# Ranking in PSUM, full-width matmuls and a single grid instruction in an early-fusion kernel

## The reference

```
h = concat(tokens(x), txt)                       # 192 x 64 for each of 16 examples
h = h + softmax(LN(h) LN(h)^T / 8) LN(h)
z = LN(h); w = z wr + br                         # router: one number per token
sel = the 95 tokens with the largest w           # top 96, of which 95 are used
h = h + z + [w * (gelu(z w1 + b1) w2 + b2) for tokens in sel, 0 elsewhere]
h = h + causal attention of 16 heads of 64, one key head, window 128, RoPE, RMS norm
z = LN(h); e = argmax(z rout + rb)               # one of 32 experts
h = h + relu(relu(z W1[e] + b1[e]) W2[e] + b2[e])
```

## Time and profile before

| | us |
|---|---|
| median of 3 runs (579.9 to 582.99) | 582.66 |
| the profiled execution | 583.62 |
| its span, first to last instruction | 581.8 |
| PE busy, of the span | 502.2 (86%) |
| DVE busy | 417.8 (72%) |
| ACT busy | 311.9 (54%) |
| POOL busy | 234.7 (40%) |
| granted TensorE clock, mean | 0.971 |

### The profile page before, as it was taken

How to read it: one execution, slowest core, us unless ns; L and a number is a source line. 1 busy time by engine, 2 the same in 40 slices (tenths; PEclk the granted TensorE clock), 3 DMA queues, 4 the chain that set the end, 5 groups by cost and what they waited for, 6 DMA issues and landing times.

```text
span 581.8 us, 14569 instructions
## 1 busy us (share of the span) xinstructions
PE 502.2 (86%) x5920; PEld 386.4 (66%) x5920; DVE 417.8 (72%) x1291; ACT 311.9 (54%) x593; POOL 234.7 (40%) x217
## 2 busy tenths in 40 slices
PE   3457499879999899989998999899989999899845
PEld 2235277658867786778776877688767767777622
DVE  3669766996799769976997699957995697363220
ACT  1414346565667556766577565756575655454311
POOL 2316632554446342643454436354462446420000
PEclk9999999989999999999998999899999999999966
DMA  7000000000000000000000000000000000000000
GB/s 271 1 6 0 1 7 2 3 1 7 3 2 10 7 2 2 10 7 3 2 9 3 2 3 2 8 3 2 3 10 2 2 2 9 2 3 9 2 1 7
DMA packets 6450, 6.29 MB, mean 11 GB/s; under 512 B 4208, under 2 KB 5744, under 8 KB 6256
## 3 DMA queue, kind: packets, MB, share of 16 engines
q1 hardware_dynamic: 6384, 5.37, 3.0%
HBM read 4.31 MB, written 0.79 MB: 9 GB/s over the span
## 4 chain that ended last, share of the span: by engine, by line
PE 47%; DVE 35%; ACT 9%; POOL 2%; issue 2%; DMA 2%; SPq 1%; POOLq 0%; ACTq 0%; DVEq 0%
PE bank L961 38%; PE bank L979 10%; DVE eq L515 5%; DVE negm L631 4%; DVE q_sb L568 4%; DVE ssq L585 4%; DVE tb L568 4%; DVE on L648 3%; ACT qT L810 3%; POOL qs L793 2%; DMA p<-masks 2%; DVE eq L506 1%; ACT qs L810 1%; DVE eq L431 1%; DVE rec L644 1%
## 5 line engine op out<-in xcount | busy, mean ns | idle before, releaser
L631 DVE TENSOR_REDUCE negm<-bank 128x2 f32<-128x384 f32 (+1 forms) x128 | 79.2, 619 | 39.6 <-PE bank L961 38.4
L793 POOL TENSOR_TENSOR qs<-q_sb,qs 128x1024 fp32r<-128x1024 f32 x24 | 56.8, 2368 | 107.8 <-ACT qs L810 107.8
L919 ACT ACTIVATE p<-bank 128x512 f32<-128x512 f32 x112 | 66.0, 599 | 56.6 <-PE bank L961 55.4
L961 PE MATMUL bank<-kh,qT 128*128 128x128 f32 (+1 forms) x384 | 82.0, 323 | 0.0
L810 ACT ACTIVATE qT<-bank 128x512 fp32r<-128x512 f32 x96 | 54.3, 596 | 50.3 <-PE bank L979 49.9
L961 PE MATMUL bank<-vx,p 128*64 128x65 f32 x1536 | 68.8, 225 | 1.3 <-DVE on L648 1.2
L961 PEld LDWEIGHTS bank<-vx,p 128*64 128x64 f32 x1536 | 60.5, 138 | 13.9 <-issue 6.8
L756 POOL TENSOR_TENSOR q_sb<-q_sb,tb 128x512 f32<-128x512 f32 x24 | 36.5, 1519 | 74.3 <-DVE tb L568 74.3
L961 PEld LDWEIGHTS bank<-kh,qT 128*128 128x128 f32 x384 | 64.2, 199 | 2.1
L961 PE MATMUL bank<-sh_r,sh_l 128*128 128x512 f32 x112 | 53.2, 475 | 0.0
L644 DVE RECIPROCAL rec<-bank 128x4 f32<-128x4 f32 (+1 forms) x88 | 15.7, 179 | 48.4 <-PE bank L961 48.0
(11 more groups left out here) (158 smaller groups left out, 1122.9 us busy)
## 6 DMA issues: line engine op xcount, KB each, us to landing
wts<-weights SPq DMA_DIRECT2D x1, 1313.5 KB, 7.3
h<-txt SPq DMA_DIRECT2D x1, 672.0 KB, 8.4
img<-images SPq DMA_DIRECT2D x8, 72.0 KB, 1.9
q_sb<-wqkv SPq DMA_DIRECT2D x1, 576.0 KB, 9.7
sh_r<-mT SPq DMA_DIRECT2D x32, 4.0 KB
out<-o_sb SPq DMA_DIRECT2D x8, 64.0 KB, 1.9
p<-masks SPq DMA_DIRECT2D x1, 480.0 KB, 10.4
cst<-shapes SPq DMA_DIRECT2D x1, 304.0 KB, 3.8
```

Of the source, the lines that this page charges most:

```text
L631: ve.tensor_reduce(dst, src, AX_X, ALU.max, negate=True).then_inc(s_vec, 1)
L793: gp.tensor_tensor(qs[:, :, D:2 * D], ta[:, t, 0:NH, :], qs[:, :, 0:D].bitcast(F32), ALU.subtract).then_inc(b_pool, 1)
L919: ac.activation(dst.rearrange("s h t -> s (h t)"), bank[BANK_E[n % 2]][:, :], ACT.Exp).then_inc(e_act, 1)
L961: return pe.matmul(dst, lhsT, rhs, start=start, stop=stop, skip_group_check=True)
```

## The change

Three things are changed, and the tables of order are made anew for all engines.

1. `rt` is no longer a tile in SBUF but a view of bank 4. The router's bias comes in as a row of the weights against a row of ones in `xaT` (one more memset at the start). ACT's step `route` is gone. The ranking waits for PE, and `h1a` waits for the ranking, since it writes the same bank. In the order of A `rank2` and `rank3` now stand ahead of `h1a`.
2. `s01`, `route`, `h1a`, `h1b`, `logits` and the experts' `h0` to `h3` are written as one matmul of 128 columns in place of two of 64. The products with 64 or 65 moving columns (`ctx`, `y`, `V`, `wo`, `out`) stay in halves.
3. The step `cols` writes four 32-row products side by side, and one DVE instruction makes the grid; the constant `resize` has 32 columns instead of 128.

```diff
-FIRST_COLS = dict(ident=128, resize=128, own_j=8, tok=64, tokb=64)
+FIRST_COLS = dict(ident=128, resize=32, own_j=8, tok=64, tokb=64)
-A_ORDER = [..., "xT2", "route", "rank1", "h1a", "rank2", "h1b", "rank3", "y", "h"]
+A_ORDER = [..., "xT2", "route", "rank1", "rank2", "rank3", "h1a", "h1b", "y", "h"]
...
-    "pe": "A15 B4 A B A B A B A B A2 B2 A2 B2 A S A B A B S A S B S B2 S A S B A S E2 S B2 A S B2 V S B A S B V S B "
+    "pe": "A15 B3 A2 B2 A B A B2 A2 B2 A B2 A S B2 S A S B2 S A B A B S A S2 E2 B S B2 A S B2 V S B S B A S E V S B "
...
-        rt = sb("rt", [P, 2, T])
-            ve.memset(xaT[D:P, :], 0.0)
+            ve.memset(xaT[D:P, :], 0.0).then_inc(set_ones, 1)
+            ve.wait_ge(set_ones, 1)
+            ve.memset(xaT[D:D + 1, :], 1.0)
...
-                for o in range(4):
-                    m = slice(32 * o, 32 * o + 32)
-                    ins = ve.tensor_tensor(grid[m, :, :, :], f[m, :, o, :].unsqueeze(3).broadcast_to([32, 2, 8, 8]),
-                                           cs("own_j")[m, :].unsqueeze(1).unsqueeze(1).broadcast_to([32, 2, 8, 8]), ALU.mult)
+                ve.tensor_tensor(grid, f.unsqueeze(3).broadcast_to([P, 2, 8, 8]),
+                                 cs("own_j").unsqueeze(1).unsqueeze(1).broadcast_to([P, 2, 8, 8]), ALU.mult).then_inc(a_vec, 1)
...
+            rt = bA[:, 0:2 * T].rearrange("q (b t) -> q b t", b=2)
             def a_rank1(p):
-                ve.wait_ge(a_act, after(A_ACT, p, "route"))
+                ve.wait_ge(a_pe, after(A_PE, p, "route"))
...
-                ("A", "route"): a_do(["route"], rt[:, :, :].rearrange("q b t -> q (b t)"), bA[:, 0:2 * T], ACT.Identity,
-                                     bias=wt("br")),
...
             def a_cols(p):
-                halves(bA[:, 0:2 * 32], cs("resize")[0:IMG, :], z_sb, True, True).then_inc(a_pe, 1)
+                z = z_sb.rearrange("c (b o i) -> c b o i", b=2, o=4)
+                for o in range(4):
+                    ins = mm(bA[32 * o:32 * o + 32, 0:16], cs("resize")[0:IMG, :], z[:, :, o, :], True, True)
+                ins.then_inc(a_pe, 1)
...
             def a_route(p):
-                    halves(bA[:, T * b:T * b + P], wt("wr"), xfT[:, c0], True, True)
-                    ins = halves(bA[:, T * b + P:T * b + T], wt("wr"), xfT[:, c1], True, True)
+                    mm(bA[:, T * b:T * b + P], wt("wr"), xfT[:, c0], True, True)
+                    ins = mm(bA[:, T * b + P:T * b + T], wt("wr"), xfT[:, c1], True, True)
...
             def a_h1(c):
-                    pe.wait_ge(a_act, after(A_ACT, p, ["route", "h1a"][c]))
-                    halves(bA[:, 0:PT], wt("w1")[:, P * c:P * c + P], xfT[:, :], True, True).then_inc(a_pe, 1)
+                    if c == 0:
+                        pe.wait_ge(a_vec, after(A_VEC, p, "rank"))
+                    else:
+                        pe.wait_ge(a_act, after(A_ACT, p, "h1a"))
+                    mm(bA[:, 0:PT], wt("w1")[:, P * c:P * c + P], xfT[:, :], True, True).then_inc(a_pe, 1)
```

More of the change, by code:

```diff
@@ L38 @@
 SHAPE_COLS = dict(rope=192, iota=32, before=384)
-FIRST_COLS = dict(ident=128, resize=128, own_j=8, tok=64, tokb=64)
-WEIGHT_COLS = dict(wo01=512, wo2=512, w1=256, w2=128, wr=128, br=1, b1=2, b2=64, qn=64, kn=64,
+FIRST_COLS = dict(ident=128, resize=32, own_j=8, tok=64, tokb=64)
+WEIGHT_COLS = dict(wo01=512, wo2=512, w1=256, w2=128, wr=128, b1=2, b2=64, qn=64, kn=64,
                    rout=32, rb=32, e1=512, e2=256, e2b=64)
@@ L61 @@
 A_PE = ["rows", "cols", "tok", "xT1", "s01", "s2", "ctx", "xT2", "route", "h1a", "h1b", "y"]
-A_ACT = ["rows", "xT1", "p01", "p2", "xT2", "route", "h1a", "h1b"]
+A_ACT = ["rows", "xT1", "p01", "p2", "xT2", "h1a", "h1b"]
 B_VEC = (["sums", "stats", "xn", "hi", "xs", "r00", "r01", "ssq00", "r10", "ssq01", "r11", "ssq10", "r20", "ssq11",
@@ L117 @@
     + [f"S{n}" for n in range(8, 16)] + ["mT2"]
-A_ORDER = ["rows", "cols", "tok", "ln1", "xn1", "xT1", "s01", "s2", "ctx", "ln2", "xn2", "xT2", "route", "rank1", "h1a", "rank2", "h1b",
-           "rank3", "y", "h"]
+A_ORDER = ["rows", "cols", "tok", "ln1", "xn1", "xT1", "s01", "s2", "ctx", "ln2", "xn2", "xT2", "route", "rank1", "rank2", "rank3", "h1a",
+           "h1b", "y", "h"]
 W_ORDER = ["eye", "shr0", "mask", "shr1", "wq", "shr2", "shr3"]
@@ L826, in f @@
                 def f(p):
-                    if p.n == 0 and name[0] == "route":
+                    if p.n == 0 and name[0] == "h1a":
                         ac.wait_ge(ld_w, 16)
@@ L856, in b_kv @@
                 if p.n == 0:
-                    ac.wait_ge(set_ones, 1)
+                    ac.wait_ge(set_ones, 2)
                 copy(vx[p.par][:, :, 0:D], b[:, 0:2, D:2 * D])
@@ L990, in a_rows @@
                 for b in range(2):
-                    ins = mm(bA[0:IMG, 32 * b:32 * b + 32], img[p.par][:, b, :], cs("resize")[0:IMG, 0:32], True, True)
+                    ins = mm(bA[0:IMG, 32 * b:32 * b + 32], img[p.par][:, b, :], cs("resize")[0:IMG, :], True, True)
                 ins.then_inc(a_pe, 1)
@@ L1016, in a_s01 @@
                 if p.n == 0:
-                    pe.wait_ge(set_ones, 1)
+                    pe.wait_ge(set_ones, 2)
                 for b in range(2):
                     c0, c1 = cols(b)
-                    halves(bA[:, T * b:T * b + P], xaT[:, c0], xaT[:, c0], True, True)
-                    ins = halves(bA[:, T * b + P:T * b + T], xaT[:, c0], xaT[:, c1], True, True)
+                    mm(bA[:, T * b:T * b + P], xaT[:, c0], xaT[:, c0], True, True)
+                    ins = mm(bA[:, T * b + P:T * b + T], xaT[:, c0], xaT[:, c1], True, True)
                 ins.then_inc(a_pe, 1)
@@ L1247, in d_logits @@
                 for t in range(NT):
-                    ins = halves(bD[:, EXPERTS * t:EXPERTS * t + EXPERTS], xdT[:, P * t:P * t + P], wt("rout"), True, True)
+                    ins = mm(bD[:, EXPERTS * t:EXPERTS * t + EXPERTS], xdT[:, P * t:P * t + P], wt("rout"), True, True)
                 ins.then_inc(d_pe, 1)
@@ L1257, in f @@
                     pe.wait_ge(d_act, after(D_ACT, p, ["oneT", "h0", "h1", "h2"][c]))
-                    halves(bD[:, 0:PT], wt("e1")[:, P * c:P * c + P], xdT[:, :], True, True).then_inc(d_pe, 1)
+                    mm(bD[:, 0:PT], wt("e1")[:, P * c:P * c + P], xdT[:, :], True, True).then_inc(d_pe, 1)
                 return f
@@ L1332, in shape_constants @@
     c["before"] = (j < own).reshape(P, 2 * T)
-    c["resize"] = np.tile(np.concatenate([haar_resize(), np.zeros((P - IMG, 32))], 0), (1, 4))
+    c["resize"] = np.concatenate([haar_resize(), np.zeros((P - IMG, 32))], 0)
     return {n: a.astype(np.float32) for n, a in c.items()}
@@ L1352, in packed_weights @@
     c["w2"] = w["L0_ffn_w2"].reshape(2, P, D).transpose(1, 0, 2).reshape(P, 2 * D)
-    c["wr"] = rows(np.repeat(w["L0_ffn_wr"], P, 1))
-    c["br"] = np.repeat(w["L0_ffn_br"].reshape(1, 1), P, 0)
+    c["wr"] = rows(np.repeat(np.concatenate([w["L0_ffn_wr"], w["L0_ffn_br"].reshape(1, 1)], 0), P, 1))
     c["b1"] = w["L0_ffn_b1"].reshape(2, P).T
```

3 lines of the change are left out of this document (1 added, 2 removed), and 62 rows, old and new, of the table MERGE.

## The result

The changed kernel took 585.16 us (median of 6 runs, 584.32 to 586.09) against 581.33 us (6 runs, 579.64 to 582.99): ratio 1.0055, interval 1.003 to 1.0081. It is slower by about half a per cent. The forecast was 570.5, faster: it is wrong in sign, and 585.16 lies outside both its own range (564 to 577) and the range for 8 in 10 (556 to 583).

A forecast was written before the change was run, and what follows sets the result against it. PE was taken to have least room (busy 58.24 of 60.70 us). Terms summed to -10.5, then +1.5 for early windows and -3 for DVE's stretch: 583.6 to 571.6, median 570.5; range 564 to 577, 8 in 10 556 to 583.

The forecast's parts named there:

- Changes of width: On PE, 98 fewer switches between 128 and 64 columns, at 0.175 us each: -17.1 us.
- wider products: On PE, router, `s01` and logits as full-width products cost +0.80 us a pair, +6.4 over 8 pairs.
- DVE's waits: Hold-up moves from `rank2` to `xf` and `kk`; PE's waits change by -0.3 for each of six pairs: -2 us.
- DVE's stretch: In the long DVE stretch, less DVE work and shorter PE answers give -0.5 a pair: -3 us over six.
- Products of 384 columns: On PE, one full-width product takes as long as its two halves, 2 x 0.32 us: 0.
- PSUM as a source: DVE's ranking reads PSUM in 11 instructions per pair at no extra cost: 0.
- Grid: Four DVE instructions become one, 0.85 us less per pair, counting only in the first pair: -0.9 us.
- First pair: `h1a` waits for the ranking, +3.2; `s01` and router at half clock, +0.4; with the grid +2.7 us.
- End: Last D steps, one by one at half clock, have wider logits and weights: +0.7 us.
- Clock: With less idling, one of two clock drops that follow the ranking's idle time may go: -1.2 us.
- (d): PE's gain in the DVE stretch goes unused, with `xf` held up and PSUM reads 65 ns dearer: 582 us, chance 0.06.
- (c): Ranking and hold-ups in series on DVE make PE wait 5 us a pair at `kTh` and `h1a`: 592 us, chance 0.12.

The follow-up runs named there:

- after_no_long_pool: The changed kernel with GpSimd's multiplication and subtraction on one head of sixteen in every pair but the first: 569.7 us, ratio 0.9795 to the kernel before.
- new_order_alone: The kernel before with only the changed kernel's order of steps, ACT's copy of `rt` put behind `xT2`: 591.1 us, ratio 1.0155.
- grouping_alone: The kernel before with `rank2` and `rank3` right behind `rank1` in every pair, ranking still in SBUF: 602.4 us, ratio 1.035.

## Why the prediction was wrong

Two things failed. The largest term, PE's changes of width, was counted and priced too high and then credited for the whole pair, though DVE set more than half of it. And the exchange of hold-ups on DVE was taken to be a gain, when more of them came than went. The loss against the kernel before, 3.8 us, is a third thing: in the profiles the start and the end grew by 1.5 and 1.6 us, and the stretch between gained back one of the two. Point by point, by the prediction's own terms:

- **Changes of width (-17.1) and wider products (+6.4).** The largest miss: -10.7 forecast. The wide products alone, -6.9 of it by my count, measured 0 in the new order, +2 (not told from 0) in the old, and 0.2 us a pair with PE as the bound. Three reasons. The price: 0.25 for there and back where I read 0.35; I summed the delays at a border as if none of them overlapped. The count: 88 fewer instead of 98, and 54 instead of 76 for the wide products. By an estimate from both, 54 x 0.125 = 6.8 us come in for the wide products and 6.4 go out for their length, which is the nothing that was measured; for the whole change it is 88 x 0.125 - 6.4 = 4.6 us. And the place: 33.7 of 60.4 us of the pair were DVE's, where PE's time is not the bound. I saw the chain change sides, and then counted PE's gains over the whole pair, since PE looked nearly full. It was "busy" 57.9 us of 60.4 and 58.2 of 60.7, but by its pieces the chain was DVE's for half of it or more in both; in `after_no_long_pool`, where the chain is PE's for 44 us, it is 57.3 of 58.1. A share of 96% did not say which engine set the pair.
- **DVE's waits (-2).** Here the mechanism failed. I saw the hold-up move to `xf` and `ks`, and sized both rightly (1.8 forecast and 1.7 measured; 0 to 2 and 1.3). I did not see the third, `wsel`, at 1.5: I took an instruction of three columns for free. And I priced them by PE's waits, 1.3 us a pair, instead of by the length of DVE's stretch. Two of the three, 3.2 us of DVE, were worth 2.1 us a pair and 13.1 in all. PE's waits themselves came out near my figure, 1.7 a pair: 0.9 at V9 and 0.8 at `xT2`, none of note at `kTh` or `h1a`.
- **DVE's stretch (-3).** The balance of what went and came was wrong: 4.5 us of hold-up came for the 3.3 at `rank2`, not 1.8 for 3.3. With the long POOL steps taken away both kernels gain about the same, 15.5 and 15.7 us, so the change neither won nor lost much by them.
- **Products of 384 columns: 0.** Right: 0.67 to the next product (at 279.85) for the 0.64 forecast. **Router and logits:** 0.91 (of 0.88 forecast) and 0.64 (0.66): right.
- **PSUM as a source: 0.** Right: `rank2` and `rank3` take 414 and 416 ns from PSUM; `rank1` 283. By my estimate from the Trainium skill ("VectorE: DVE Perf Modes", section "The TRN2 errata — SBUF-src ops pay a fixed extra latency per instruction") they should be 65 ns dearer each. In this case's rows they are not: `rank3` takes 412 ns from SBUF before, 416 from PSUM after.
- **Grid (-0.9).** Too small: 3.6 us alone. That DVE's 0.85 a pair is mostly hidden in the steady pair was right (0.2 came out), and so nearly were 0.9 at the start (1.1). What I put at nothing is the shorter constant, which brings the first pair forward by 1.2 us.
- **First pair (+2.7).** First `m0` 3.75 later. By the first `negm` 1.5 of it are left. The ranking's 3.9 is right. What was missing is the table load of 1.28 us, which I had counted only as a gain on ACT (17 of 29 loads, as forecast). The copy of `rt` had been what it hid behind: in pair 0 that step also waited for the weights, and this wait now stands ahead of `h1a`, with the load behind it. The shorter constant took 1.2 us off again.
- **End (+0.7).** It was 1.6. At the low clock full width is dearer: 1.65 us against 1.55 for a product of 384 columns, 1.49 against 0.86 for the logits. With halves the end is 35.0. **Clock (-1.2).** The two drops behind the ranking did go. But in the early window the clock is 0.78 instead of 1.00. Of the kernel before the ten runs with a mean clock of 0.947 took 583.4 to 585.1 us and the three with 0.979 took 579.6 to 581.1, so this term can be as large as the whole result. Over all runs the means of the two kernels are 0.957 and 0.959, which gives no reason for the difference.
- **The rivals.** (d), the DVE stretch sets it, was the nearest with 0.06. Its first reason, DVE's stretch with `xf` held up, was right, its second, dearer reads of PSUM, was not, and its size (582) is short by the start and end. (c) had the right sign and the wrong place: its wait at `h1a` came only in the old order. I gave them 0.18 together, and 0.68 to cases in which PE's work counts in full.

Without the hold-ups at `xf` and `wsel` the steady pair is 58.4 us, just the 58.3 I had forecast for the changed kernel. That is chance: it comes from 2.1 us of DVE, not from PE's widths.

`wsel` follows the rule of the Trainium skill, "SBUF — State Buffer", section "SBUF: two separate sides": of VectorE and GpSimd whoever starts first gets the shared pair of ports for the whole instruction, and the other is blocked. With two SBUF inputs it is held to the end of `lo0`; with one of them in PSUM it takes 0.16 beside the same `lo0`. I had quoted the rule, and applied it to long instructions only.

What stays open: what the new order costs without the late copy of `new_order_alone`, how `grouping_alone` loses so much beyond its 3.39 us of wait, and the 2.3 us by which the medians differ more than the profiles.

## What to carry to other kernels

When the chain of waits changes sides within a period, a saving counts only in the stretch of the engine it is on; an engine that is busy 95% of the time may be following. Before moving VectorE work, list for every instruction with two SBUF inputs, or of the form of `xf` here (2.48 us for 0.75), which long GpSimd instruction will run beside it: the one of three columns was held for 1.45 us, as long as the others. The cure is small: a sum into spare PSUM columns, or GpSimd's dependent step put ahead of its long one. A step that is removed may have been the cover of something else, here a table load in the first pair. And look at what else an edit changes: here a smaller constant gave more of the start's gain than the instructions that were merged.
